# Dealing the output-projection matmuls out among the attention and score matmuls

## The reference

```python
x = layernorm(x + autocorrelation(x))
h_q = (rmsnorm(x) * ln_weight) @ w_q.T     # 1024 x 4096, 32 heads of 128
h_k = ctx @ w_k.T
h_v = ctx @ w_v.T
score = einsum('bqhd,bkhd->bhqk', h_q, h_k) + position_bias
score = softmax(where(mask, score, -inf))
attn = einsum('bhqk,bkhd->bqhd', score, h_v)
x = layernorm(x + x + attn @ w_out.T)
x = layernorm(x + ffn(x))
```

## Time and profile before

| | |
|---|---|
| three runs | 1072.99, 1074.5, 1075.21 us; median 1074.5 |
| span of the profiled execution | 1071.4 us |
| between the span and the median of the runs | 3.1 us |
| PE busy | 1037.1 us, 97% of the span, 5946 matmuls |
| weight loads | 903.5 us, 84% |
| DVE / ACT / POOL busy | 659.0 / 458.9 / 313.4 us |
| mean granted TensorE clock | 0.988 of full speed |

### The profile page before, as it was taken

One profiled execution on the slowest core, in us unless ns is written; L12 is line 12 of the kernel. 1 busy time (PEld: TensorE's weight loads), 2 busy tenths in 40 slices (PEclk: granted clock), 3 DMA queues, 4 the chain that ended last, 5 costly groups with the idle time before them and its releaser, 6 DMA issues.

```text
span 1071.4 us, 16826 instructions
## 1 busy us (share of the span) xinstructions
PE 1037.1 (97%) x5946; PEld 903.5 (84%) x5946; DVE 659.0 (62%) x1189; ACT 458.9 (43%) x1090; POOL 313.4 (29%) x236
## 2 busy tenths in 40 slices
PE   8989999999999999999999999999999999799995
PEld 7778888888888888888888888888888888578784
DVE  5766666666666666666666666666666666853615
ACT  6866343434343434343434343434343434254251
POOL 1645040404040404040404040404040402343204
PEclk9999999999999999999999999999999999899998
DMA  9402020202020202020202020202020300300011
GB/s 299 134 1 84 2 84 1 83 0 83 0 83 0 83 0 83 0 83 0 83 0 83 0 83 0 83 0 83 0 83 0 122 1 20 109 21 1 1 40 40
DMA packets 20698, 52.39 MB, mean 49 GB/s; under 512 B 3136, under 2 KB 7232, under 8 KB 20672
## 3 DMA queue, kind: packets, MB, share of 16 engines
q1 hardware_dynamic: 20672, 52.06, 14.6%
HBM read 49.95 MB, written 2.10 MB: 49 GB/s over the span
## 4 chain that ended last, share of the span: by engine, by line
PE 88%; DVE 5%; POOL 2%; ACT 2%; issue 1%; DMA 1%; DVEq 0%; SPq 0%; POOLq 0%; ACTq 0%
PE psum L1330 25%; PE psum L1332 25%; PE psum L1331 25%; PE psum L1336 8%; PE psum L1337 3%; PE psum L1463 3%; DMA raw<-in_dft 1%; POOL rows L511 1%; DVE st L1045 0%; PE psum L1568 0%; DVE wts L1012 0%; POOL stat L581 0%; DVE rsum L1240 0%; ACT xn_hi L647 0%; POOL stat L583 0%
## 5 line engine op out<-in xcount | busy, mean ns | idle before, releaser
L539 POOL TENSOR_TENSOR smx<-far,bias 128x512 f32<-128x512 f32 x64 | 82.7, 1292 | 423.2 <-DVE smx L1068 421.5
L735 ACT ACTIVATE smx<-smx,nmax 128x128 f32<-128x128 f32 x256 | 99.8, 391 | 231.8 <-DVE nmax L1074 231.8
L976 DVE TENSOR_TENSOR qk<-psum,qk 128x512 fp32r<-128x512 f32 x136 | 93.2, 687 | 105.1 <-ACT qk L647 105.1
L1330 PE MATMUL psum<-wv_lo,cx_hi 128*128 128x256 f32 x512 | 149.7, 292 | 0.3 <-DVE xn_lo L976 0.3
L1332 PE MATMUL psum<-wv_hi,cx_hi 128*128 128x256 f32 x512 | 144.5, 282 | 0.0
L1331 PE MATMUL psum<-wv_hi,cx_lo 128*128 128x256 f32 x512 | 144.5, 282 | 0.0
L647 ACT ACTIVATE qk<-psum 128x512 fp32r<-128x512 f32 x136 | 80.8, 596 | 140.7 <-PE psum L1332 140.6
L976 DVE TENSOR_TENSOR vv_lo<-psum,vv_hi 128x512 fp32r<-128x512 f32 x64 | 44.2, 691 | 124.9 <-ACT vv_hi L647 124.9
L489 POOL TENSOR_TENSOR wqk_lo<-raw,wqk_hi 128x1024 fp32r<-128x1024 f32 x31 | 74.3, 2396 | 127.8 <-ACT wqk_hi L647 127.8
L1330 PE MATMUL psum<-wo_lo,at_hi 128*128 128x512 f32 x256 | 105.9, 414 | 1.1 <-issue 1.1
L1330 PE MATMUL psum<-cx_lo,wqk_hi 128*128 128x512 f32 x256 | 100.3, 392 | 1.8 <-DVE wqk_lo L976 1.8
(11 more groups left out here) (184 smaller groups left out, 2351.7 us busy)
## 6 DMA issues: line engine op xcount, KB each, us to landing
raw<-in_wqk SPq DMA_DIRECT2D x32, 512.0 KB, 3.4
raw<-in_wv SPq DMA_DIRECT2D x16, 512.0 KB, 4.3
raw<-in_wo SPq DMA_DIRECT2D x16, 512.0 KB, 3.3
raw<-in_ffn SPq DMA_DIRECT2D x10, 512.0 KB, 3.3
raw<-in_dft SPq DMA_DIRECT2D x7, 512.0 KB, 4.6
acc<-in_x SPq DMA_DIRECT2D x2, 1024.0 KB, 9.1
raw<-in_ctxT SPq DMA_DIRECT2D x4, 512.0 KB, 10.2
bias<-in_bias SPq DMA_DIRECT2D x32, 64.0 KB, 1.8
```

The lines of the kernel that those rows point to most:

```text
L539: nc.gpsimd.tensor_tensor(bm, far[:, HB * hf:HB * hf + HB, :], g_, ALU.add).then_inc(s_bm_ready, 1)
L735: a.activation(exps[:, b, :], scores_sb[:, b, :], ACT.Exp, bias=nmax[:, 1, b:b + 1], accum_out=esum[:, 0, b:b + 1]).then_inc(s_exp_done, 1)
L976: return v.tensor_tensor(dst, src, hi, ALU.subtract)
L1330: mm(out, lhs(0), rhs(1), start=first, stop=False)
```

## The change

The six matmuls of `outputs(n-2)` for i = 0 are put, one by one, among the eight short matmuls of `attend(n)`, and the six for i = 1 among those of `scores(n+1)`. The number and shape of the matmuls stay as they are. `attend` and `scores` are cut into their two halves, `values` and `outputs` into pieces. It applies in all units from 2 to 62. In unit 1, which has no outputs yet, `scores` now comes ahead of `attend`; DVE's order there is turned round in the same way. On DVE, ACT, POOL and SP nothing else moves.

```diff
+            def attend_hi(j, b):
                 hp, hf = j % 2, j // 2
+                mm(psA[:, b], vv[0][:, HB * hf + b, hp * P:(hp + 1) * P], pt_parts[:, :, b, :], start=True, stop=False)
+
+            def attend_lo(j, b):
+                hp, hf = j % 2, j // 2
+                last = mm(psA[:, b, 1], vv[1][:, HB * hf + b, hp * P:(hp + 1) * P], pt[0][:, b, :],
+                          start=False, stop=True)
+                if b == HB - 1:
+                    last.then_inc(s_a_mm, 1)
...
+            def score_lo(b):
+                bk = slice(b * P, (b + 1) * P)
+                last = mm(psS[:, b, 1], qk[1][:, 0, bk], qk[0][:, 1, bk], start=False, stop=True)
+                if b == HB - 1:
+                    last.then_inc(s_scores_mm, 1)
...
+            def output_term(o, first_tile, i, k):
+
+                hf, tile, hp = first_tile // HB, (first_tile + i) % HB, k // 3
+                lhs, rhs = ((0, 1), (1, 0), (0, 0))[k % 3]
+                last = mm(out_banks(o)[i][:, :], at[lhs][:, hf, hp, tile * P:(tile + 1) * P], wo[rhs][:, hp, :],
+                          start=k == 0, stop=k == 5)
+                if k == 5:
+                    last.then_inc(s_o_mm, 1)
...
+            def attend_and_output(n, g, j, o, first_tile):
+
+                attend_ready(n, g, j)
+                output_bank(o, 0)
+                attend_hi(j, 0)
+                output_term(o, first_tile, 0, 0)
+                attend_lo(j, 0)
+                output_term(o, first_tile, 0, 1)
...
+                output_term(o, first_tile, 0, 4)
+                attend_lo(j, 2)
+                attend_hi(j, 3)
+                output_term(o, first_tile, 0, 5)
+                attend_lo(j, 3)
+
+            def scores_and_output(n, o, first_tile):
+
+                scores_ready(n)
+                output_bank(o, 1)
+                score_hi(0)
+                output_term(o, first_tile, 1, 0)
+                score_lo(0)
...
+                score_hi(3)
+                output_term(o, first_tile, 1, 5)
+                score_lo(3)
...
+                    else:
+                        turn_probs(n)
+                        if not (last and j == 2):
+                            values(n + 2, g + (j >= 2), tile)
+                            value_tile(tile, 1)
+                        if is_first(g) and j == 1:
+                            scores(n + 1)
+                            attend(n, g, j)
+                        else:
+                            outputs_ready(n - 2, g - (j < 2), tile)
+                            attend_and_output(n, g, j, n - 2, tile)
+                            scores_and_output(n + 1, n - 2, tile)
```

The DVE order of a unit in the loop, written out in the new branch:

```diff
+                    else:
+                        attended(n, j)
+                        softmax_in(n + 1)
+                        add_out(n - 2, 0, (2 * ((j + 2) % 4)) % B)
...
+                        softmax_out(n + 1)
+                        add_out(n - 2, 1, (2 * ((j + 2) % 4) + 1) % B)
```

More of the change, by code:

```diff
@@ L1196, in pair_dve @@
                               value_dst(0, j + 2))
-                    attended(n, j)
                     if is_first(g) and j == 0:
+                        attended(n, j)
                         xt_lo(4)
                         xt_lo(5)
-                    if front:
                         softmax_in(n + 1)
-                    if is_first(g) and j == 0:
                         xt_lo(6)
                         xt_lo(7)
[L1206 to L1214, removed]
-                        softmax_out(n + 1)
+                        softmax_out(n + 1)
+                    elif is_first(g) and j == 1:
+                        softmax_in(n + 1)
+                        attended(n, j)
+                        softmax_out(n + 1)
+                    elif last and j == 3:
+                        attended(n, j)
+                    else:
+                        attended(n, j)
+                        softmax_in(n + 1)
+                        add_out(n - 2, 0, (2 * ((j + 2) % 4)) % B)
+                        if last and j == 2:
+                            ffn_lo(UP[3])
+                        softmax_out(n + 1)
+                        add_out(n - 2, 1, (2 * ((j + 2) % 4) + 1) % B)
             every_pair(dve, pair_dve)
@@ L1332, in mm3 @@
                 return mm(out, lhs(0), rhs(0), start=False, stop=last)
-            def mm_parts(out, lhs, rhs_both, rhs_hi):
-                mm(out, lhs(0), rhs_both, start=True, stop=False)
-                return mm(out[:, 1], lhs(1), rhs_hi, start=False, stop=True)
             def dft(hf):
@@ L1436, in values, with value_tile, score_hi, scores_ready @@
                     pe.wait_ge(s_o_add, 2 * m - 8)
[L1437 to L1444, removed]
+                value_tile(first_tile, 0)
+            def value_tile(first_tile, i):
+                tk = slice((first_tile + i) * P, (first_tile + i + 1) * P)
+                for c in range(DC):
+                    last = mm3(psV[:, i * 2 * P:(i + 1) * 2 * P], lambda i_: cx[i_][:, c, tk],
+                               lambda i_: wv[i_][:, c, :], c == 0, c == DC - 1)
+                if i == 1:
+                    last.then_inc(s_v_mm, 1)
+            def score_hi(b):
+                bk = slice(b * P, (b + 1) * P)
+                mm(psS[:, b], qk[0][:, 0, bk], qk_parts[:, :, 1, bk], start=True, stop=False)
+            def score_lo(b):
+                bk = slice(b * P, (b + 1) * P)
+                last = mm(psS[:, b, 1], qk[1][:, 0, bk], qk[0][:, 1, bk], start=False, stop=True)
+                if b == HB - 1:
+                    last.then_inc(s_scores_mm, 1)
+            def scores_ready(n):
                 pe.wait_ge(s_q_lo, n + 1)
@@ L1450, in scores @@
                     pe.wait_ge(s_stats_a, HB + 1)
+            def scores(n):
+                scores_ready(n)
                 for b in range(HB):
-                    bk = slice(b * P, (b + 1) * P)
-                    last = mm_parts(psS[:, b], lambda i: qk[i][:, 0, bk], qk_parts[:, :, 1, bk], qk[0][:, 1, bk])
-                last.then_inc(s_scores_mm, 1)
+                    score_hi(b)
+                    score_lo(b)
             def turn_probs(n):
@@ L1464, in turn_probs, with attend_ready @@
                 last.then_inc(s_t_mm, 1)
-            def attend(n, g, j):
+            def attend_hi(j, b):
                 hp, hf = j % 2, j // 2
+                mm(psA[:, b], vv[0][:, HB * hf + b, hp * P:(hp + 1) * P], pt_parts[:, :, b, :], start=True, stop=False)
[5 more added lines that the diff above has]
+                    last.then_inc(s_a_mm, 1)
+            def attend_ready(n, g, j):
+                hf = j // 2
                 pe.wait_ge(s_t_lo, n + 1)
@@ L1474, in attend, with outputs_ready @@
                     pe.wait_ge(s_general, 2)
+            def attend(n, g, j):
+                attend_ready(n, g, j)
                 for b in range(HB):
[L1476 to L1480, removed]
+                    attend_hi(j, b)
+                    attend_lo(j, b)
+            def outputs_ready(o, g, first_tile):
                 hf = first_tile // HB
@@ L1488, in outputs, with output_bank @@
                     pe.wait_ge(s_a_lo, 4 * g + 2 + 2 * hf)
-                for i in range(2):
[L1490 to L1507, removed]
+            def output_bank(o, i):
+                if isinstance(o, int) and o in LATE:
+                    pe.wait_ge(s_q_lo, units)
+                    pe.wait_ge(s_k_lo, units)
+                    pe.wait_ge(s_scores_full, units)
+                    pe.wait_ge(s_o_add, 2 * (o - 2) + i + 1)
+                else:
+                    if i == 0:
+                        pe.wait_ge(s_k_lo, min(o + 4, units) if isinstance(o, int) else o + 4)
+                    else:
+                        pe.wait_ge(s_v_lo, min(o + 5, units) if isinstance(o, int) else o + 5)
+                    if isinstance(o, int) and due(2 * (o - 1) + i + 1):
+                        pe.wait_ge(s_o_add, 2 * (o - 1) + i + 1)
@@ new lines, in output_term, with outputs @@
+            def output_term(o, first_tile, i, k):
[5 more added lines that the diff above has]
+                    last.then_inc(s_o_mm, 1)
+            def outputs(o, g, first_tile):
+                outputs_ready(o, g, first_tile)
+                for i in range(2):
+                    output_bank(o, i)
+                    for k in range(6):
+                        output_term(o, first_tile, i, k)
@@ L1515, in _ @@
             values(0, 0, 0)
+            value_tile(0, 1)
             for tile in range(HB - 1):
@@ L1521, in _ @@
             values(1, 0, 2)
+            value_tile(2, 1)
             project(0, 0, 0, 0)
@@ L1524, in _ @@
             values(2, 0, 4)
+            value_tile(4, 1)
             scores(0)
+            def attend_and_output(n, g, j, o, first_tile):
+                attend_ready(n, g, j)
+                output_bank(o, 0)
[3 more added lines that the diff above has]
+                output_term(o, first_tile, 0, 1)
```

(46 more changed lines are left out.)

## The result

The changed kernel takes 1115.39 us (1113.62 to 1116.71, four runs) beside 1073.74 us for the kernel before (1072.33 to 1075.21, four runs). The ratio is 1.0386 with a 95% interval of 1.0366 to 1.0405: 42 us slower. The forecast was 1107.5 with a range of 1084 to 1117; the time lies inside it, near its upper end, and 0.4 us above the range that the likeliest case had for itself.

A forecast was written before the change was run, and what follows sets the result against it. PE's own stream was taken to bound the loop; reordering costs nothing, K's stall 60 times 0.55 gives 33 us, head and tail cancel: span 1071.4 becomes 1104.4, plus 3.1 is 1107.5 us, range 1084 to 1117.

The forecast's parts named there:

- the likeliest case: The forecast of 1107.5 us itself, from K's stall in the loop; chance 0.70, own range 1102 to 1115.
- The mechanism: In the loop, late scores delay softmax_in by 1.65 us, add_out behind it on DVE, so K waits 0.55 us.
- slower still: Rival: ACT's late copy makes attended hold softmax_in 0.2 us in all or some units; 1112 to 1125 us; chance 0.07.
- Both rivals that wanted a shorter block: 128-column matmuls hide: 24 us less, 1083 to 1100, chance 0.14; block at pure streaming: 1061, chance 0.04.
- the stall of 0.55 us: At K's first matmul in each unit: 1.65 us shift less 1.10 in hand; bounds 0.50 to 0.65.
- DVE reacts 0.03 later: At softmax_in: DVE starts 0.03 us after the scores end, 4.72 us into the block, so at 4.75.
- DVE's way to PE: From add_out's end on DVE to K's start on PE: 0.17 us, or 0.12 at the lower bound.
- The other links: Last score matmul 4.50 us into the block; add_out behind softmax_in in DVE's in-order queue.
- the head: Unit 1's exchange may remove PE's 1.29 us stall at unit 2: -1.3 at best, 0 at worst.
- the tail: Behind the last block, unit 63's probabilities come later: +1.65 us at worst, 0 if something hides it.
- Covered, by 0.3 us: Attention result, about 1.4 us later: DVE finishes attended 0.3 us before the scores end, so no wait.
- It still comes in time: Second bank, freed by add_out(n-2, 1) for V: shifted by 1.65 us, V by 0.55, so V doesn't wait.

The follow-up runs named there:

- Experiment 2: Changed kernel with nothing dealt: attend, then all twelve output matmuls, then scores, each in one piece; 1112.56 us, ratio 1.0361.
- 3: Changed kernel with the last one of the 12 dealt-out output matmuls put behind the last score matmul; 1102.97 us, ratio 1.0273.
- experiment 6: Kernel before, with the low-part matmuls of attend and scores at 256 columns in place of 128; 1075.56 us, ratio 1.0007.
- experiment 1: Changed kernel with add_out of the first tile moved ahead of attended and softmax_in on DVE; 1091.72 us, ratio 1.0173.
- Experiment 9: Changed kernel with scores dealt first, attend second; DVE does attended last, ACT the exponentials ahead of its attention-result copy; 1078.63 us, ratio 1.0036.
- Experiment 4: Changed kernel with the last three of the 12 dealt-out output matmuls put behind the last score matmul; 1092.77 us, ratio 1.018.
- experiment 8: Changed kernel with three dealt-out outputs put behind the scores and first-tile add_out moved ahead of attended on DVE; 1072.34 us, ratio 0.9981.

## Why the prediction was right, and where its size was off

- *The mechanism held.* 60 waits at K's first matmul, released by `add_out`; L1068 released by the last score matmul; no wait at the transposes in the loop. Experiment 2 shows that the late scores alone make it, 3 that it follows their end one for one. The rival "slower still" named 1112 to 1125 us, and the measured time lies there too, but not by that rival's way: it wanted `attended` to hold `softmax_in` up. After, L1068 waits for PE in all 60 units of the loop (62 times in all, where it did so once before), and for 0.2 to 0.3 us each time, so DVE was through with `attended` earlier:

```profile
DVE smx L1068 <- PE psum L1452: 18.3, 62, 0.3
```

- *The short matmuls hide nothing.* From the 128-column matmul at 524.00 to the true start of its long successor (524.11) are 0.11 us, and the block of 28 takes 4.64 us against 4.63 forecast. Both rivals that wanted a shorter block fall, and experiment 6 shows the same 0.12 at twice the columns. The Trainium skill ("TensorE: Matmul & The Clock Gate", Back-to-back issue gap) states about 81 ns for a matmul of 128 columns in a stream of loads and matmuls. This trace doesn't agree with it: 0.11 us among long neighbours, 0.117 among short ones.
- *The step that was mis-sized is the stall of 0.55 us.* It stood on "DVE reacts 0.03 later, as it did at 81.20 after a matmul ending at 81.17". In the loop the scores end at 527.68 and L1068 starts at 527.82: 0.14, and 0.13 in experiment 1 (516.12 to 516.25). The row that I took lies where the granted clock was 0.50 (80 to 82 us), its matmul is recorded with 0.31 us in place of 0.22, and the ends of matmuls are modelled: it doesn't carry over. Which of these makes the difference was not separated. I gave bounds to DVE's way to PE, which was right at 0.17 (530.80 to 530.97), and none to PE's way to DVE. The other links were right: the last score matmul 4.52 us into the block (4.50 forecast), 2.98 from `softmax_in` to the end of `add_out`.
- *The account.* The 0.11 more of reaction and the 0.02 by which the last score matmul stands later in the block, less the 0.01 by which Q does, put K 0.67 later behind Q than the 2.72 of before, where 0.55 was forecast; 0.01 and 0.02 lie in the other two stretches: 0.70 a unit, 42 us in 60 units where 33 were forecast. To this come 1.6 us gained in the head (scores of unit 0 to transposes of unit 2: 33.96 before, 32.40 after) and 1.5 lost in the tail (from there to the end: 971.0 before, 1014.5 after, less the 42). These two I had let cancel, as they nearly did; the gain is 0.3 beyond its bound of 1.3, the loss inside its bound of 1.65. Another 1.5 us are those by which the scores of unit 0 start sooner (64.92 against 66.44), ahead of anything that was changed. 42 - 1.6 + 1.5 - 1.5 are the 40.4 us between the spans.
- *Dealing out is not quite free.* I costed it at zero, and the block itself did cost nothing. Experiment 9 shows 0.07 us a unit behind it, in Q. After, Q is as slow (527.58 to 530.37 for twelve, 2.79) but K's wait covers it.
- *What stood right behind.* "Covered, by 0.3 us" for `attended` was right, and the size nearly so. After, DVE could begin its next operation at 527.43 (526.82 and the 0.61 from start to start): 0.25 ahead of the scores' end, and 0.39 ahead of the start of L1068. Experiment 4 bears this out: it brings the scores 0.69 nearer and gives back 0.39 of it (14.08 to 13.69), until `attended` is in the way. "It still comes in time" for the second bank was right only because K was late too: take K's wait away, and V waits (experiment 1).

## What to carry to other kernels

Where an engine is full, the order of its instructions is worth what it does to the time of the results, not to their number: follow each moved result through the in-order engine that takes it, to whatever else stands in that queue, here a bank's release that had nothing to do with the scores. Count the slack of the next two or three waits as well, because removing the first (experiments 1 and 4) gave back only 55 and 53% of the loss, by the ratios. A reaction time is to be read from a row at the clock and in the stage where it will be spent.

## What the runs showed of the hardware that was not expected

- Twelve long matmuls straight behind a dealt-out block run at 0.232 us each (2.79 for Q's twelve in experiment 9, and after), where the same twelve behind other long ones run at 0.227. That the block ends in a short matmul is not enough: in experiment 2 Q stands straight behind eight short ones in one piece, and goes from 472.21 to 474.71 in eleven distances, 0.227 each. With three long matmuls between the block and Q (experiment 8) Q takes 2.72 us again, from 506.31 to 509.03 on PE:

```profile
506.31 0.39 PE L1333 MATMUL psum<-xn_lo,wqk_hi 128*128 128x512 f32 x1
...
509.03 0.39 PE L1333 MATMUL psum<-cx_lo,wqk_hi 128*128 128x512 f32 x1
...
511.75 0.60 PE L1477 MATMUL psum<-ident,smx 128*128 128x128 f32 x4
...
519.68 0.39 PE L1333 MATMUL psum<-xn_lo,wqk_hi 128*128 128x512 f32 x1
```

Why the distance stays long for a whole dozen was not found.

- A matmul of 128 columns costs as much as one of 256 (0.117 and 0.120 us, experiment 6), so a doubled product of this shape cost nothing that the runs can tell (1.0007).
